# Expert stage written out slot by slot: gathers issued ahead of stores, two banks for the down products, rows normalised on ScalarE

## The reference

```python
def reference(x, tok.., attn.., ffn..):
    # patches of 16 steps, stride 8; layer norm with gamma, beta; times W; plus b      -> h [16, 255, 256]
    h = _L0_tok_ref(x, L0_tok_W, L0_tok_b, L0_tok_gamma, L0_tok_beta)
    # gated linear attention, 8 heads, a scan over the 255 tokens; times W_o
    h = h + _L0_attn_ref(_layernorm(h, axis=-1), ...)
    h = h + _L0_ffn_ref(_layernorm(h, axis=-1), ...)

def _L0_ffn_ref(hidden_states, w_red, wg, W1, b1, W2, b2):
    logits = (x @ w_red) @ wg_n.T            # 8 experts
    gates = jax.nn.softmax(logits, axis=1)
    scores, idx = jnp.max(gates, axis=1), jnp.argmax(gates, axis=1)
    h = x @ W1[idx] + b1[idx]                # 256 -> 512, by the token's own expert
    h = jax.nn.gelu(h, approximate=False)
    o = h @ W2[idx] + b2[idx]                # 512 -> 256
    return (o * scores[:, None]).reshape(b, t, c)
```

## Time and profile before

| | |
|---|---|
| median of 3 runs | 576.51 us (574.85 to 576.92) |
| the profiled execution | 576.19 us, span of its trace 574.4 us |
| busy share of the span | PE 90%, PEld 64%, DVE 80%, ACT 40%, POOL 34% |
| mean granted TensorE clock | 0.979 of 2.4 GHz |
| expert stage | about 408 us to the end |

### The profile page before, as it was taken

One profiled execution on the slowest core, in us unless ns is written; L12 is line 12 of the kernel. 1 busy time (PEld: TensorE's weight loads), 2 busy tenths in 40 slices (PEclk: granted clock), 3 DMA queues, 4 the chain that ended last, 5 costly groups with the idle time before them and its releaser, 6 DMA issues. The chain is left out here.

```text
span 574.4 us, 12975 instructions
## 1 busy us (share of the span) xinstructions
PE 516.6 (90%) x3425; PEld 366.1 (64%) x3426; DVE 460.2 (80%) x1220; ACT 231.1 (40%) x447; POOL 197.0 (34%) x285
## 2 busy tenths in 40 slices
PE   2989999999999999999889889998688898998982
PEld 1876667777666777666645677774365575665651
DVE  2668888898888898888988989999577887777771
ACT  1335545465545455654445312221043344443440
POOL 7452232322132223123211112221425655655532
PEclk9999999999999999999989979999799999999997
DMA  9311211221221220221130334435312222222210
GB/s 249 111 37 38 75 48 62 73 62 48 73 73 37 73 73 37 73 73 37 38 98 29 85 87 117 113 88 201 105 30 70 71 65 70 73 59 68 61 44 0
DMA packets 34985, 41.99 MB, mean 73 GB/s; under 512 B 8514, under 2 KB 26163, under 8 KB 34704
## 3 DMA queue, kind: packets, MB, share of 16 engines
q1 hardware_dynamic: 24908, 27.06, 15.7%
q0 software_dynamic: 3744, 9.34, 5.7%
q10 hardware_dynamic: 6308, 5.28, 3.2%
HBM read 32.97 MB, written 9.59 MB: 74 GB/s over the span
## 5 line engine op out<-in xcount | busy, mean ns | idle before, releaser
L521 PE MATMUL banks<-proj,xnT_h 128*128 128x512 f16 x384 | 114.5, 380 | 1.5 <-DVE early L1226 1.5
L502 PE MATMUL banks<-early 128*128 128x256 f16 x768 | 86.8, 273 | 2.5 <-DVE wo_l L1055 2.5
L502 PEld LDWEIGHTS banks<-early 128*128 128x128 f16 x768 | 75.1, 98 | 11.1 <-DVE wo_l L1055 2.7
L521 PE MATMUL banks<-proj,xnT_l 128*128 128x512 f16 x192 | 72.8, 379 | 0.0
L521 PEld LDWEIGHTS banks<-proj,xnT_h 128*128 128x128 f16 x384 | 37.6, 98 | 37.6 <-DVE early L1226 2.0
L1865 POOL DMA_INDIRECT out<-proj,vo x39 | 39.8, 1021 | 63.0 <-DVE vo L1688 38.1
L750 PE MATMUL banks<-w2h,vo 128*128 x312 | 57.7, 273 | 3.6 <-DVE proj L1686 2.6
L731 PE MATMUL banks<-w1h,vo 128*128 x156 | 53.8, 386 | 7.4 <-issue 4.7
L1859 POOL DMA_INDIRECT vo<-token_rows,vo x39 | 43.1, 1105 | 27.8 <-issue 27.8
L1002 ACT ACTIVATE vo<-banks 128x256 f16<-128x256 f32 x39 | 14.9, 383 | 89.7 <-PE banks L718 65.2
L1797 POOL TENSOR_TENSOR w1l<-stage,w1h 128x512 f32 (+1 forms) x16 | 18.9, 1183 | 83.7 <-ACT w1h L885 83.7
(11 more groups left out here) (261 smaller groups left out, 1261.4 us busy)
## 6 DMA issues: line engine op xcount, KB each, us to landing
early<-in_x SPq DMA_DIRECT2D x16, 512.0 KB, 3.4
stage<-in_W SPq DMA_DIRECT2D x32, 256.0 KB, 2.8
early<-lam_by_chunk SPq DMA_DIRECT2D x32, 68.0 KB
token_rows<-rows ACTq DMA_DIRECT2D x16, 129.0 KB, 2.4
early<-lam_by_head SPq DMA_DIRECT2D x16, 128.0 KB, 3.1
rows<-in_b SPq DMA_DIRECT2D x1, 2048.0 KB, 7.4
token_rows<-rows ACTq DMA_DIRECT2D x16, 112.9 KB, 2.1
vo<-in_tok_W ACTq DMA_DIRECT2D x2, 512.0 KB, 7.3
```

The costliest lines, as they stand in the source:

```text
L502: last = mm(bank(2 + j, D), x_[:, k, at:at + P], w[:, KG * half + k, :], start=(half == 0 and k == 0 and x_ is gT_h and w is wtok_h), stop ...
L521: last = mm(dst, a, c, start=(i == 0), stop=(i == n - 1))
```

## The change

1. TensorE's, ScalarE's, VectorE's and GpSimd's 39 slots are written out; no loop is left in the expert stage. Each expert number is read once and kept in its register until down(i).
2. GpSimd waits for slot i's result, gathers for slot i+6 first and stores slot i then. The row numbers are taken straight from `gather_id` and `store_id`; VectorE's copy of row numbers (L1688) and the semaphore `y_done` are gone.
3. Down products of even slots go to bank 3, of odd slots to bank 6, so that down(i) waits for finish(i-2) and not for finish(i-1).
4. `norm_rows` moves from VectorE to ScalarE, as one activation with scale and bias from the table's two columns. So the table holds -mean x scale and scale, and GpSimd makes them in the mixing stage: `roots2` takes two tiles at a time, with three instructions, in place of `root2` with one tile and one instruction.
5. ScalarE's list within a slot becomes split_rows(i+1), split_gelu(i-1), gelu(i), norm_rows(i+2); before it was split_rows(i+1), gelu(i), split_gelu(i-1).

The diff, cut:

```diff
@@ tensor
             def down(i, w, e):
 
                 pe.wait_ge(s["g_done"], i + 1)
-                if not (isinstance(i, int) and i == 0):
-                    pe.wait_ge(s["y_steps"], i)
+                if i >= 2:
+                    pe.wait_ge(s["y_steps"], i - 1)
...
-                        last = mm(bank(3, D), a[:, w, f, :], ...
+                        last = mm(bank(3 + 3 * w, D), a[:, w, f, :], ...
...
-            def slots(g, count=RING, first=False, last=False):
-
-                i0 = RING * g
-                experts = {0: expert_of(i0)}
-                for w in range(count):
-                    up(i0 + w, experts[w])
-
-                    if w + 1 < count:
-                        experts[w + 1] = expert_of(i0 + w + 1)
-                    if w < 2 and not first:
-                        experts[w - 2] = expert_of(i0 + w - 2)
...
-            with pe.Fori(1, ROUNDS) as g:
-                slots(g)
...
+            experts = {0: expert_of(0)}
+            for i in range(SLOTS):
+                up(i, experts[i])
+                if i + 1 < SLOTS:
+                    experts[i + 1] = expert_of(i + 1)
+                    transpose_rows(i + 1)
+                if i >= 1:
+                    transpose_gelu(i - 1, (i - 1) % 2)
+                if i >= 2:
+                    down(i - 2, i % 2, experts[i - 2])
@@ scalar
+            def norm_rows(i):
+                g, w = divmod(i, RING)
+                act.wait_ge(s[f"row_in_{w}"], 16 * g + 16)
+                if i >= 1:
+                    act.wait_ge(s["xdt_ready"], i)
+                af(xnD, xr[:, w, 2:ROWC], ACT.Identity, bias=xr[:, w, 0:1], scale=xr[:, w, 1:2]).then_inc(s["xd_ready"], 1)
...
+            for i in range(SLOTS):
+                if i + 1 < SLOTS:
+                    split_rows(i + 1)
+                if i >= 1:
+                    split_gelu(i - 1, (i - 1) % 2)
+                gelu(i, i % 2)
+                if i + 2 < SLOTS:
+                    norm_rows(i + 2)
@@ vector
-            def norm_rows(i, w, g):
-                dve.wait_ge(s[f"row_in_{w}"], 16 * g + 16)
...
-                ts(xnD, xr[:, w, 2:ROWC], xr[:, w, 0:1], xr[:, w, 1:2], ALU.subtract,
-                   ALU.mult).then_inc(s["xd_ready"], 1)
...
             def scaled_bias(i, w, e):
                 row = xr[:, w, 2:ROWC]
+                dve.wait_ge(s["xd_ready"], i + 1)
...
-                copy(ring_ids[:, w, :], slot_ids[:, bass.ds(i, 1), :].rearrange("p a v -> p (a v)")).then_inc(s["y_done"], 1)
@@ gpsimd
-            def root2(t):
-                pool.wait_ge(s["h2_steps"], 3 * t + 3)
-                var = rows[:, bass.ds(t, 1), 1:2].rearrange("p a b -> p (a b)")
-                ptt(var, var, minus_half[:, 0:1], ALU.pow).then_inc(s["rstd2_ready"], 1)
...
+            def roots2(n):
+                pool.wait_ge(s["h2_steps"], 3 * (2 * n + 1) + 3)
+                mean = rows[:, bass.ds(2 * n, 2), 0]
+                var = rows[:, bass.ds(2 * n, 2), 1]
+                ptt(mean, zeros[:, 0:2], mean, ALU.subtract).then_inc(s["root2_done"], 1)
+                ptt(var, var, minus_half[:], ALU.pow).then_inc(s["root2_done"], 1)
+                pool.wait_ge(s["root2_done"], apart(pool, 2 * n + 2))
+                ptt(mean, mean, var, ALU.mult).then_inc(s["rstd2_ready"], 2)
...
+            pool.wait_ge(s["slot_ids_ready"], 1)
+            for i in range(SLOTS):
+                pool.wait_ge(s["y_steps"], i + 1)
+                if i + RING < SLOTS:
+                    load(i + RING)
+                store(i)
```

More of the change, by code:

```diff
@@ L238, in build @@
         gather_id = over(SLOTS).bitcast(I32)
[L239 to L240 removed]
+        store_id = over(SLOTS).bitcast(I32)
         sloti = over(SLOTS).bitcast(I32)
@@ L784, in _ @@
+            transpose_gelu(SLOTS - 1, (SLOTS - 1) % 2)
+            for i in (SLOTS - 2, SLOTS - 1):
+                down(i, i % 2, experts[i])
         @block.scalar
@@ L1659, in split_gelu @@
                 dve.wait_ge(s["gh_done"], i + 1)
-                if not (isinstance(i, int) and i < 2):
+                if i >= 2:
                     dve.wait_ge(s["m2_ready"], i - 1)
@@ L1685, in finish @@
                     dve.wait_ge(s[f"y_out_{w}"], 16 * g)
[L1686 removed]
+                stt(yo[:, w, :], bank(3 + 3 * (i % 2), D), slot_score[:, bass.ds(i, 1)], xr[:, w, 2:ROWC], ALU.mult,
                     ALU.add).then_inc(s["y_steps"], 1)
[L1688 to L1704 removed]
@@ L1720, in _ @@
+            split_gelu(SLOTS - 1, (SLOTS - 1) % 2)
+            finish(SLOTS - 2)
+            finish(SLOTS - 1)
         @block.gpsimd
```

130 lines of the change are left out of this document (39 added, 91 removed).

## The result

The changed kernel took **570.33 us** in the median of 6 executions (569.45 to 584.79), the kernel before 575.51 (574.15 to 576.92, 6). The ratio is 0.9901 with a 95% interval of 0.9879 to 0.9924: 1.0% less, 5.7 us where 16.8 were forecast.

What follows compares the result with a forecast made beforehand. TensorE was taken to bound the kernel, with 16.96 us of excess in the expert slots. -16.96 - 1.5 + 0.18 + 1.5 = -16.8 us, from 576.19 to 559.4 us; range 556.5 to 565.

Steps and rivals of the forecast that it cites:

- What bounds, and 3.26 us a slot: Expert slots: TensorE's 24 matmuls back to back take 3.26 us a slot, and no ordering goes below it.
- Slots written out, minus 16.96: Expert slots: without jumps and repeated expert-number loads, 36 slots fall from 134.32 to 117.36 us, if nothing else bounds.
- GpSimd itself needs 1.2 + 0.3 + 1.0 + 0.3 = 2.8 us a slot, below 3.26: Expert slots: GpSimd's gather and store issues with their gaps fit within TensorE's time for a slot.
- 3.5 us a slot: Expert slots: the chain of copy, store, gather and normalising would hold this pace if the jumps alone were removed.
- The two slots from 487.70: Middle of a loop round before the change: gather and store both run, TensorE busy for 6.50 of 6.50 us.
- VectorE "loses 0.41 and 0.16 a slot": Expert slots: VectorE, busy for 10.89 of 13.10 us, gives up the normalising (0.41) and the row-number copy (0.16).
- Normalising on ScalarE, 0.59: Expert slots: one activation of 0.59 us, delaying no split; exposed once at the first rows, plus 0.18 us.
- Gathers ahead of stores: Expert slots: gathered rows land at 14.7 us, ScalarE wants them at 16.3, so 1.6 us of slack.
- Two banks, minus 1.5: End of the expert stage: the last down products no longer wait for the previous finish, 1.5 us earlier.
- Mixing stage, plus 1.5: Pair roots delay ScalarE's store and the vo copy behind it in the second tile group; 1.5 us, between 0.3 and 2.3.
- rival 5: Expert slots: gathers still set the pace, 3.5 us a slot and more, to 570, chance 0.03; no change (576), 0.01.
- Both signs named for a wrong prediction: Slots starting 3.4 us apart or more, or the stage before them longer by over 3 us.

Runs made afterwards that it cites:

- norm_dve: The changed kernel, but VectorE normalises and roots are taken tile by tile, as in the kernel before; ratio 0.9769 to the kernel before.
- norm_dve_one_bank: norm_dve with one bank instead of two for the down products; ratio 0.9802 to the kernel before.
- pause: The changed kernel plus one idle GpSimd root (0.55 us) between a slot's store and the next gather; ratio 0.9753 to the kernel before.
- pause_tile_roots: pause with the table's roots and scaled means taken tile by tile instead of pair by pair; 559.09 us, ratio 0.9699 to the kernel before.
- again: The changed kernel run once more, nothing edited; median 573.1 us, ratio 0.9874 to the kernel before.
- norm_dve_table: The changed kernel with pair roots and the table's scale and bias kept, but VectorE applies them; ratio 0.9831 to the kernel before.
- paced: The changed kernel, but GpSimd issues a slot's gather and store only after TensorE's count for that time's up products; some 3.5 us gained on the changed kernel.
- gated: norm_dve with each store issued only once TensorE's count for the next slot's down products has come; ratio 0.9802 to the kernel before.

## Why the prediction was wrong, step by step

- **What bounds, and 3.26 us a slot**: right as a floor. Six kernels reach 3.26 or 3.27 from slot 2 to 38, and none goes below.
- **Slots written out, minus 16.96**: the jumps and loads went as said (39 loads), but the term took for granted that nothing else bounds. "GpSimd itself needs 1.2 + 0.3 + 1.0 + 0.3 = 2.8 us a slot, below 3.26" is the step that failed. I read it as room enough, and it is the very case, issues 0.3 apart, in which TensorE's counts come late. The slots came out at 3.93 in the first trace and 3.77 in the second, and a pause added to GpSimd's round, nothing else, brings them to 3.26 and the kernel 7.0 to 8.5 us down: with the 2.1 us by which the mixing stage was set too low, 9.1 to 10.6 of the 11.1 us that are missing. Writing the slots out alone gave 2.8 us, for the reason that the prediction did name (3.5 us a slot; 3.62 measured). The two slots from 487.70, in which gather and store run and TensorE has no gap, did not speak against this: the kernel before has a pause of 1.06 us or more in each round of GpSimd from the third on. What that pause was good for was not to be seen in it, since the view of waits names no count that is late.
- **VectorE "loses 0.41 and 0.16 a slot"** was booked as relief at no cost. In the first slots it brings the finish's end, and so GpSimd's wake-up, forward from 1.1 to 1.5 us into the slot (norm_dve) to 0.8 to 1.1, and soon one comes before the store's issue has ended: short pauses start at slot 6 and are 15 where norm_dve has 8. That the earlier finish is what brings them on is read from the traces, not tested by itself.
- **Normalising on ScalarE, 0.59**: right, 588 ns in the median. That it stands last in ScalarE's list was called harmless; with late counts it stands behind the wait for one, and TensorE idles 1.4 us for it every second slot. Moving it up gained nothing measurable.
- **Gathers ahead of stores**: the slack was right, no wait of ScalarE for rows beyond the first; in norm_dve they are worth 6.0 us, which lifts the limit of 3.5 us a slot that the prediction had worked out.
- **Two banks, minus 1.5**: agrees, though not closely shown: 1.9 by norm_dve_one_bank with overlapping intervals, and from slot 38's up product to the end 17.1 us where the kernel before has 19.1. TensorE's last product waits 0.2 us.
- **Mixing stage, plus 1.5**: mechanism and place right, size wrong. 3.6 us by the norm_dve pair, 3.1 by pause and pause_tile_roots, 3.2 in the trace. The chain took 1.40 us from first operation to ready, where 1.2 was taken; between it and the copy I put 0.1, and it was 0.44 with ScalarE's issue of the row store. Behind it TensorE's matmuls ran at the lower level, 1.2 GHz, for longer than in the kernel before (10.2 us against 6.8 from tile 3's statistics to the last; the pair L661 took 1.08 us). Granted clock, columns as in the earlier trace rows:

```profile
326.00:336.00 10.00, 6.63 (x30) 5.06 (x30) 6.83 (x21) 1.72 (x5) 1.23 (x3) 0.83 0.17 53
336.00:346.00 10.00, 9.88 (x39) 8.25 (x40) 8.11 (x33) 1.54 (x4) 2.27 (x6) 0.66 0.31 81
```

  In the kernel before the same two stretches have 0.80 and 0.86. The wait came first, the low level behind it. But the clock is the smaller part. From tile 3's statistics to the last of the stage, the traces with pair roots that have the least time at the lower level (again, norm_dve_table, pause) take 68.0 to 68.8 us, the seven with roots by tile and as little of it 64.9 to 65.6. So the pairing costs some 3.0 us at an equal clock, and the longer low level in the changed kernel's trace about 0.5 more. In its other pairs the wait was hidden, as said; in the traces of pause and paced another 1.4 us (tiles 7 to 15) and 2.3 us (tiles 15 to 23) were lost, and why is open.
- **The rivals**: rival 5 gave 570, the time that came, by another mechanism (GpSimd's transfers do set the pace, though the gather itself is shorter than before, 1.03 us). A rival by which relief of one engine crowds another's issues was missing. Both signs named for a wrong prediction, slots over 3.4 and a stage longer by over 3, were seen.
- That pause_tile_roots takes 559.1 us, and 559.4 is on record, is in part luck: with the mixing stage's 1.5 gone the sum on record would give 557.9, and its slow first slots make up for the rest.

**What stays open.** Why TensorE's counts are held when a third issue follows closely, and no other engine's (in the changed kernel's trace VectorE's and ScalarE's recorded counts in the slots are all within 0.02 us); the runs show when and not how. Every execution compared here has a recorded span and clock, so no run tells whether recording takes part. The changed kernel's executions of about 570 us were never the traced ones; that they have fewer short pauses is an argument, not shown. And lags of up to 0.6 us stay behind long pauses, which the pause does not explain.

## What to carry to other kernels

An engine's round that fits into the slot by its sum can still be too full: look at the pauses between its DMA issues, and at what the pauses hang on, before you shorten the work that feeds it. When an engine idles behind matmuls that have ended, compare the matmul's end with the moment at which its count was raised; if they differ, the cause is at neither engine of the wait. And where two items are batched for one operation, price every in-order queue that waits for the pair, with the DMA issues that stand between.

## What the runs showed of the hardware

- TensorE's counts came up to 2.57 us after the end of their matmuls while the work went on. With both kinds of indirect transfer in the slots, a count over 0.6 us late stood beside each pause under 0.6 us between one slot's second issue and the next slot's first, in the kernels with nothing added to GpSimd's list: 64 of 64 with gathers ahead, 22 of 22 with stores ahead. In gated it was 21 of 28. Behind a pause of 0.78 or more none was later than 0.601. With only one kind: 0 of 303 counts late by over 0.02 us.
- GpSimd's indirect issue of 128 rows takes 0.98 to 1.04 us in the changed kernel's slots (single ones up to 1.3 elsewhere), the next follows 0.3 later where nothing is waited for, and 0.80 to 0.82 after VectorE's finish where it waited for that.
- One root of 0.57 us in each slot on an engine that was 50% busy made the whole kernel 7.0 to 8.5 us faster.
- A pair of tiles batched for one power, with ScalarE's in-order stores between, cost 3.0 us in the mixing stage at an equal clock (68.0 to 68.8 us against 64.9 to 65.6 from tile 3's statistics to the last).
